# A two-layer graph attention kernel: its setup in another order, query and key weights first

## The reference

```python
q, k, v = (proj(Wq, bq), proj(Wk, bk), proj(Wv, bv))        # x @ W.T + b, in heads
scores = jnp.einsum('bhqd,bhkd->bhqk', q, k) / np.sqrt(D_HEAD)
mask = adj + jnp.eye(n, dtype=adj.dtype)[None] > 0
attn = jax.nn.softmax(jnp.where(mask[:, None], scores, -jnp.inf), axis=-1)
out = jnp.einsum('bhqk,bhkd->bhqd', attn, v)                 # then heads joined
h = x + out @ Wo.T + bo
x1 = (h - mu) * jax.lax.rsqrt(var + EPS) * gamma + beta
feat_proj = x1 @ fc_w.T + fc_b
logits = (feat_proj @ q_w.T + q_b) + (feat_proj @ k_w.T + k_b).swapaxes(2, 1)
masked = logits + (1.0 - adj) * NEG_INF
masked = jnp.where(masked >= 0, masked, LEAKY_SLOPE * masked)
y = jax.nn.softmax(masked, axis=-1) @ feat_proj + x1
```

## Time and profile before

| | |
|---|---|
| median of 3 runs | 985.23 us (985.12 to 985.61) |
| the profiled execution: its time / its span | 985.61 us / 983.4 us |
| PE / PEld busy | 932.2 us (95%) / 777.8 us (79%) |
| DVE / ACT / POOL busy | 768.7 (78%) / 796.1 (81%) / 300.5 us (31%) |
| HBM read, written | 52.44 MB, 8.39 MB |

### The profile page before, as it was taken

The page is one execution under the profiler, slowest core; times in us unless marked ns, Lnnn a source line. Parts: engine busy times, 40 slices in busy tenths (PEclk is TensorE's granted clock), DMA queues, the critical chain, the costliest instruction groups (busy, mean ns, idle before and its releaser), DMA issues. The chain is left out here.

```text
span 983.4 us, 22056 instructions
## 1 busy us (share of the span) xinstructions
PE 932.2 (95%) x7432; PEld 777.8 (79%) x7432; DVE 768.7 (78%) x2012; ACT 796.1 (81%) x1900; POOL 300.5 (31%) x408
## 2 busy tenths in 40 slices
PE   4498999999999999999999999999999999999966
PEld 3276888888888888888788888878887888888755
DVE  3287987979788797978878797888879797887832
ACT  2187988989888897988889798988989898897923
POOL 0002332334333233433214243432323343232441
PEclk8699999999999999999999999999999999999988
DMA  5576856666575666657476665737666564756100
GB/s 150 85 110 149 118 141 108 130 119 99 136 116 133 108 130 129 109 126 117 123 119 133 123 129 109 118 124 116 150 111 129 108 108 130 118 120 108 44 22 22
DMA packets 74430, 112.59 MB, mean 114 GB/s; under 512 B 6736, under 2 KB 33360, under 8 KB 74320
## 3 DMA queue, kind: packets, MB, share of 16 engines
q1 hardware_dynamic: 74320, 111.18, 58.8%
HBM read 52.44 MB, written 8.39 MB: 62 GB/s over the span
## 5 line engine op out<-in xcount | busy, mean ns | idle before, releaser
L912 DVE CUSTOM_DVE_ANT_0 sm_bank<-sm_bank,masks 128x512 f32<-128x512 f32 x512 | 352.3, 698 | 124.1 <-PE sm_bank L494 121.2
L679 ACT ACTIVATE e<-sm_bank,row_min 128x512 f32<-128x512 f32 x512 | 355.3, 696 | 41.9 <-DVE row_min L912 41.9
L504 PE MATMUL et_bank<-ident,e 128*128 128x128 f32 x2048 | 307.9, 272 | 3.2 <-DVE e_t L920 1.9
L504 PEld LDWEIGHTS et_bank<-ident,e 128*128 128x128 f32 x2048 | 251.6, 140 | 42.5 <-issue 7.3
L494 PE MATMUL sm_bank<-k_stack,q_stack 96*128 96x512 f32 x512 | 248.0, 485 | 13.5 <-DMA k_stack<-kt_lo 12.7
L671 ACT COPY e_t<-et_bank 128x512 f32<-128x512 f32 x272 | 161.0, 592 | 16.1 <-PE et_bank L504 14.2
L920 DVE COPY e_t<-et_bank 128x512 f32<-128x512 f32 x240 | 164.4, 685 | 11.8 <-PE et_bank L504 10.2
L494 PEld LDWEIGHTS sm_bank<-k_stack,q_stack 96*128 96x128 f32 x512 | 97.2, 190 | 43.5 <-issue 25.5
L443 PE MATMUL o_bank<-e_t,v 128*32 128x256 f32 x2048 | 123.8, 382 | 0.0
L476 PE MATMUL shared<-feat,z 128*128 128x256 f32 x512 | 121.6, 381 | 0.8 <-ACT z L621 0.8
L679 ACT ACTIVATION_READ_ACCUMULATOR e<-sm_bank,row_min 128x1 f32 x512 | 106.9, 209 | 0.0
(11 more groups left out here) (110 smaller groups left out, 1578.9 us busy)
## 6 DMA issues: line engine op xcount, KB each, us to landing
adj_in<-in_adj SPq DMA_DIRECT2D x32, 1024.0 KB, 5.3
q_stack<-qt_hi SPq DMA_DIRECT2D x64, 256.0 KB, 7.1
k_stack<-kt_hi SPq DMA_DIRECT2D x64, 256.0 KB, 7.2
x_in<-in_x SPq DMA_DIRECT2D x16, 512.0 KB, 6.4
q_stack<-qt_lo SPq DMA_DIRECT2D x32, 256.0 KB, 7.1
k_stack<-kt_lo SPq DMA_DIRECT2D x32, 256.0 KB, 11.1
h<-in_x SPq DMA_DIRECT2D x16, 512.0 KB, 3.9
out_y<-h SPq DMA_DIRECT2D x32, 256.0 KB, 6.8
```

What stands on the lines that cost most here:

```text
L504: last = nc.tensor.transpose(et_bank[n % TURNED][:, c * P:(c + 1) * P], e[:, n % ROOM, c * P:(c + 1) * P], ident[:, :])
L679: nc.scalar.activation(e[:, k, :], sm_bank[n % SCORED][:, :], ACT.Exp, scale=-1.0, bias=row_min[:, k:k + 1], accum_out=row_sum[:, g, qt, i ...
L912: nc.vector.tensor_tensor_reduce(bank[:, :], bank[:, :], mask[b % 2][:, qt * N:(qt + 1) * N], 1.0, -LOWEST, ALU.add, ALU.min, row_min[:, k ...
```

## The change

SP issues Wq and Wk first (counted in a semaphore of their own, qk_loaded), then x, then the four columns of bq and bk (bias_loaded), then adj; Wv, Wo, fc_w, kw_col, the other columns and the rows follow. PE, ACT and DVE make the parts of Wq and Wk and go straight on to the turns of x and the projections k0 and q0. All the rest of the setup becomes a function other_weights on each of the three engines, called in iteration -1 at step 17, behind q0. The setup now uses the banks of the scores, of the output and of the turned tiles in place of the two shared ones, since the projections need those. The wait of SP for PE's seventh setup signal moves behind the first stack transfers, and PE waits for the whole of the setup at the first scores.

```diff
 FIRST, LAST = -1, NB + 1
+FIRST_QK, AFTER_QK = 15, 17
...
         weights_loaded, cols_loaded, const_loaded = sem("weights_loaded"), sem("cols_loaded"), sem("const_loaded")
-        N_WEIGHTS, N_COLS, N_CONST = 6, 3, 12
+        qk_loaded, bias_loaded = sem("qk_loaded"), sem("bias_loaded")
+        N_QK, N_BIAS, N_WEIGHTS, N_COLS, N_CONST = 2, 4, 4, 3, 8
         ident_made = sem("ident_made")
+        setup_banks = [*sm_bank, o_bank, et_bank[1]]
         setup_pe, setup_act, setup_dve = sem("setup_pe"), sem("setup_act"), sem("setup_dve")
...
-            for k, w in enumerate((wq, wk, wv, wo)):
+            def load_weight(k, w, signal):
                 sp.dma_start(z[:, k, 0:N].rearrange("p (o i) -> p o i", o=DT),
-                             w.rearrange("(o p) i -> p o i", p=P)).then_inc(weights_loaded, 16)
+                             w.rearrange("(o p) i -> p o i", p=P)).then_inc(signal, 16)
+
+            load_weight(WQ, wq, qk_loaded)
+            load_weight(WK, wk, qk_loaded)
+            sp.dma_start(x_in[:, :, :], rows(x, 0)).then_inc(x_loaded.sem, 16)
+            for k, b in enumerate((bq, bk)):
+                for g in range(NG):
+                    sp.dma_start(bias_col[:, k, g:g + 1], b[g * P:(g + 1) * P].rearrange("(i d) -> d i", i=GH),
+                                 allow_slow_non_contiguous=True).then_inc(bias_loaded, 16)
+            sp.dma_start(adj_in[:, :, :], rows(adj, 0)).then_inc(adj_loaded.sem, 16)
+            load_weight(WV, wv, weights_loaded)
+            load_weight(WO, wo, weights_loaded)
             sp.dma_start(h[0][:, 0:DT, :], fc_w.rearrange("(o p) i -> p o i", p=P)).then_inc(weights_loaded, 16)
             sp.dma_start(kw_col[:, :], k_w.rearrange("a (g p) -> p (a g)", p=P),
                          allow_slow_non_contiguous=True).then_inc(weights_loaded, 16)
-            sp.dma_start(x_in[:, :, :], rows(x, 0)).then_inc(x_loaded.sem, 16)
 
             for col, b in ((bias_col[:, 2, :], bv), (gamma_col[:, :], gamma), (beta_col[:, :], beta)):
                 sp.dma_start(col, b.rearrange("(g p) -> p g", p=P),
                              allow_slow_non_contiguous=True).then_inc(cols_loaded, 16)
-            for k, b in enumerate((bq, bk)):
-                for g in range(NG):
-                    sp.dma_start(bias_col[:, k, g:g + 1], b[g * P:(g + 1) * P].rearrange("(i d) -> d i", i=GH),
-                                 allow_slow_non_contiguous=True).then_inc(const_loaded, 16)
-            sp.dma_start(adj_in[:, :, :], rows(adj, 0)).then_inc(adj_loaded.sem, 16)
             for row, b in ((gamma_row, gamma), (rest_row, beta), (bo_row, bo), (fcb_row, fc_b)):
...
             def iteration(t):
                 for s in range(TILES):
+                    if t == 0 and s == 0:
+                        sp.wait_ge(setup_pe, 7)
                     if (b := due(SP_AT, "adj", s, t)) is not None and b > 0:
                         sp.wait_ge(dve_done.sem, max(dve_done.all("mask", b - 1), dve_done.all("l_max", b - 2)))
...
 
-            sp.wait_ge(setup_pe, 7)
             program(iteration)
...
             pe.wait_ge(ident_made, 2)
-            pe.wait_ge(weights_loaded, 16 * N_WEIGHTS)
-            setup_banks = [*shared, *sm_bank][:5] + [o_bank]
-            for k in range(5):
+
+            def turn_weight(k):
                 for i in range(DT):
...
                         last = nc.tensor.transpose(setup_banks[k][:, (i * DT + o) * P:(i * DT + o + 1) * P],
                                                    src, ident[:, :])
                 last.then_inc(setup_pe, 1)
-            pe.wait_ge(setup_dve, 1)
...
-            pe.wait_ge(setup_dve, 9)
+
+            pe.wait_ge(qk_loaded, 16 * N_QK)
+            turn_weight(WQ)
+            turn_weight(WK)
+
+            def other_weights():
+                pe.wait_ge(weights_loaded, 16 * N_WEIGHTS)
+                pe.wait_ge(ident_made, 4)
+                for k in (WV, WO, FC):
+                    turn_weight(k)
+                pe.wait_ge(setup_dve, 4)
+                for i in range(DT):
...
+                last.then_inc(setup_pe, 1)
+                pe.wait_ge(setup_act, 5)
+                pe.wait_ge(setup_dve, 7)
+                for kt in range(DT):
+                    for n, part in enumerate((weight_hi, weight_lo)):
...
+                last.then_inc(setup_pe, 1)
 
...
@@ -506,6 +523,13 @@
 
             def iteration(t):
                 for s in range(TILES):
+                    if t == FIRST and s == FIRST_QK:
+                        pe.wait_ge(setup_dve, 3)
+                    if t == FIRST and s == AFTER_QK:
+                        other_weights()
+                    if t == 0 and s == 0:
+                        pe.wait_ge(setup_act, 7)
+                        pe.wait_ge(setup_dve, 10)
                     if (b := due(PE_AT, "at3", s, t)) is not None:
                         attend(3, b)
...
 
         @block.scalar
         def _(act):
-            banks = [*shared, *sm_bank]
-            for k in range(4):
+
+            def high_parts(k):
                 act.wait_ge(setup_pe, k + 1)
...
+                    last = nc.scalar.copy(weight_hi[:, k, :, :], setup_banks[k][:, :].rearrange("p (i o) -> p i o", i=DT))
                 last.then_inc(setup_act, 1)
-            act.wait_ge(setup_pe, 5)
-            nc.scalar.copy(scratch[:, 6, :], banks[4][:, :]).then_inc(setup_act, 1)
...
-            act.wait_ge(const_loaded, 16 * N_CONST)
-            act.wait_ge(setup_dve, 9)
+
+            high_parts(WQ)
+            high_parts(WK)
+            act.wait_ge(setup_dve, 3)
+
+            def other_weights():
+                high_parts(WV)
+                high_parts(WO)
+                act.wait_ge(setup_pe, 5)
+                nc.scalar.copy(scratch[:, 6, :], setup_banks[FC][:, :]).then_inc(setup_act, 1)
...
+                                                scale=gamma_col[:, i:i + 1])
+                last.then_inc(setup_act, 1)
 
...
             def iteration(t):
                 for s in range(TILES):
+                    if t == FIRST and s == AFTER_QK:
+                        other_weights()
                     if (b := due(ACT_AT, "v0", s, t)) is not None:
...
-            last.then_inc(setup_dve, 1)
-            banks = [*shared, *sm_bank]
-            for k in range(4):
+
+            def low_parts(k):
                 dve.wait_ge(setup_act, k + 1)
                 if k == WQ:
...
-
-            dve.wait_ge(const_loaded, 16 * N_CONST)
-            nc.vector.tensor_scalar(bias_col[:, 0, :], bias_col[:, 0, :], -SCALE, None, ALU.mult)
-            dve.wait_ge(setup_pe, 7)
-            nc.vector.tensor_tensor(bo_row[:, :], et_bank[0][:, 0:D], bo_row[:, :], ALU.add)
...
-            nc.vector.tensor_tensor(logit_bias[:, 3:4], logit_bias[:, 0:1], logit_bias[:, 1:2], ALU.add).then_inc(setup_dve, 1)
-            dve.wait_ge(setup_dve, 13)
+
+            low_parts(WQ)
+            low_parts(WK)
+            dve.wait_ge(bias_loaded, 16 * N_BIAS)
+            nc.vector.tensor_scalar(bias_col[:, 0, :], bias_col[:, 0, :], -SCALE, None, ALU.mult)\
+                .then_inc(setup_dve, 1)
+
+            def other_weights():
+                dve.wait_ge(weights_loaded, 16 * N_WEIGHTS)
+                dve.wait_ge(ident_made, 4)
+                for o in range(DT):
+                    last = nc.vector.tensor_scalar(scratch[:, 0, o * P:(o + 1) * P], scratch[:, 1, 0:P], kw_col[:, o:o + 1], None, ALU.add)
+                last.then_inc(setup_dve, 1)
...
+                last.then_inc(setup_dve, 1)
+                low_parts(WV)
+                low_parts(WO)
+                dve.wait_ge(setup_act, 6)
+                for i in range(DT):
...
+                last.then_inc(setup_dve, 1)
+
+                dve.wait_ge(const_loaded, 16 * N_CONST)
+                dve.wait_ge(setup_pe, 7)
+                nc.vector.tensor_tensor(bo_row[:, :], et_bank[0][:, 0:D], bo_row[:, :], ALU.add)
+                nc.vector.tensor_tensor(fcb_row[:, :], et_bank[0][:, D:2 * D], fcb_row[:, :], ALU.add).then_inc(setup_dve, 1)
+                dve.wait_ge(setup_dve, 10)
...
+                nc.vector.tensor_tensor(logit_bias[:, 0:2], logit_bias[:, 0:2], qkb[:, :], ALU.add).then_inc(setup_dve, 1)
+                dve.wait_ge(setup_dve, 13)
+                nc.vector.tensor_tensor(logit_bias[:, 3:4], logit_bias[:, 0:1], logit_bias[:, 1:2], ALU.add).then_inc(setup_dve, 1)
+                dve.wait_ge(setup_dve, 14)
 
...
@@ -922,6 +963,8 @@
 
             def iteration(t):
                 for s in range(TILES):
+                    if t == FIRST and s == AFTER_QK:
+                        other_weights()
                     if (b := due(DVE_AT, "fin1", s, t)) is not None:
...
             nc.gpsimd.memset(scratch[:, 1, 0:P], 0.0).then_inc(ident_made, 1)
-            pool.wait_ge(setup_dve, 10)
+            pool.wait_ge(setup_dve, 11)
```

(20 more changed lines are left out.)

81 lines of the change are left out of this document (38 added, 43 removed).

## The result

| | before | after |
|---|---|---|
| median of the runs, us | 985.42 (985.12 to 986.05, 4 runs) | 972.78 (971.64 to 973.66, 4 runs) |
| after over before | | 0.9872, 95% interval 0.9856 to 0.9887 |
| profiled execution, us (its span) | 985.61 (983.4) | 973.40 (971.2) |
| granted clock of TensorE, mean of the profiled execution | 0.981 | 0.989 |

The kernel is 1.3% faster: 12.6 us by the medians, 12.2 by the two profiled executions (985.61 - 973.40). The forecast was 971.8, and 972.1 for the profiled execution, which came out 1.3 above it.

What follows compares the result with a forecast made beforehand. TensorE is full in the steady part, so the start adds to the whole. Taking 13.5 us off the profiled 985.61 gives 972.1, 971.7 with the 0.38 lower median; stated 971.8, range 969.3 to 975.6 us.

Steps and rivals of the forecast that it cites:

- Direction and mechanism: Start of the kernel: K and Q ahead of other setup work, first stack issue 13.5 us earlier, carried to the end.
- Weights: PE waits for Wq and Wk alone: first transpose at 4.4 us, DVE's low parts done by 7.9, bias scaled by 8.1.
- x: x issued at 1.79 us, landing at 6.5 by Wo's row; 7.6 by its own time would make K 0.7 later.
- Biases: bq and bk columns ahead of adj land at 6.7 us, no delay taken; late bound 9.3, K 1.3 us later.
- K to stack: From K's start at 10.4 us to first stack issue at 17.5: 7.1 us as before, TensorE at 0.50, SP free.
- rival B: Warm TensorE: K and Q matmuls at 0.27 us at most, not 0.42, some 2 us more off, 969.6; chance 0.10.
- Stack: From first stack issue to first scores: 14.4 us kept as before, first scores at 31.9 us.
- Block: Deferred setup behind Q: DVE done by 26.4 us, POOL by 30.0, covered by the stack transfer with 1.9 us to spare.
- After the first scores: Order unchanged and steady PE full, so the shift is carried whole; TensorE's clock may vary it 2 us either way.
- C: Rival: cover too short, or biases and x late; 976.2 us by the block, 973.1 by late bias and x; chance 0.16.
- D: Rival: slower than before, last constant landing late ahead of q1's low part and masks; 988.5 us if landed at 43; chance 0.02.
- E: Rival: nothing gained, something unseen holds the first scores at 45 us; 985.2 us, chance 0.02.

Runs made afterwards that it cites:

- experiment 1: Kernel before with only SP's setup transfers in the new order, PE, ACT and DVE in the old order; 987.06 us median, ratio 1.0026.
- experiment 2: Changed kernel with SP's setup transfers in the order of before, the engines' new order kept; 973.9 us, ratio 0.9893.
- experiment 3: Changed kernel with old transfer order and other weights' work ahead of x's turns again; only DVE's constants wait and sums behind Q; 979.1 us, ratio 0.9934.
- experiment 8: Changed kernel once more, nothing altered; 971.65 us (970.01 to 974.36, 5 runs), ratio 0.9869.
- experiment 7: Changed kernel with query bias scaling moved behind DVE's xt_lo, ACT waiting for biases only ahead of K's high part, PE not; 971.69 us, ratio 0.9865.
- experiment 5: Changed kernel with 24 chained 128x512 copies on DVE in the deferred block, ahead of its wait for the constants; 976.22 us, one run.
- 4: Changed kernel with six chained 128x512 copies on DVE in the deferred block, ahead of its wait for the constants; 972.08 us, one run.
- 6: Changed kernel with SP waiting for the four bias transfers before issuing adj and everything behind it; 974.05 us, ratio 0.9884.
- experiment 10: Changed kernel with bias off the path, first stack's query columns split, and unread transposes and matmuls filling PE's waits before K and first scores; 964.41 us, ratio 0.9791.

## Why the prediction was right, and where it was off

**Direction and mechanism** held: K ahead of the rest, the constant's wait and the block taken from the path. Experiments 1 to 3 show it part by part.

**Weights**: first transpose at 4.4, measured 4.62; DVE's low parts were done by 8.04 (7.9).

**x**: 6.5 us, chosen from Wo's place in the stream over 7.6 from x's own time; the turns began at 7.08, 6.70 (experiment 8) and 6.38 (experiment 7). The profiled execution lies halfway between the two rows, the others nearer to Wo's.

**Biases**: "I take no delay" failed in the profiled execution, and by more than its bound: scaling ended at 10.65 for 8.1, where I had allowed 1.3 us. The step at fault is the choice of bounds: 2.4 and 5.0 us were single landings, taken as if they were the ends. In experiment 5 they were late by 0.9 us, in 4, 6, 7 and 8 in time within 0.2. The Trainium skill, "DMA: Bandwidth & Descriptors", section Specifications, speaks against small pieces; of when they are late its rule tells nothing, and no run here does.

**K to stack**: 7.1 us forecast, 6.7 measured (19.40 - 12.74), since the last of Q quickened. SP was free for it, though its setup issues ended at 16.2 and not at 14.0. In experiment 8 it was 4.6, which is rival B's case: warm matmuls, and 970.01 where B had said 969.6. Whether B comes depends on the execution, not on the kernel alone; 0.10 was too low for it, as it came up in the profiles of experiments 1, 3, 6 and 8. The Trainium skill, "TensorE: Matmul & The Clock Gate", section What's actually happening, has activity release the clock; experiment 10 agrees for K, without proof that the filling did it, and only in part for the scores.

**Stack**: 14.4 forecast, 14.1 measured, 14.0 and 14.4 in experiments 7 and 8, 13.4 in 4 and 15.4 in 6. The last constants landed 2.3 us behind the first stack issue, and no delay is seen from it.

**Block**: last DVE instruction by 26.4, POOL by 30.0, with a stack issue at 17.5; measured 27.12 and 29.87 with the issue at 19.40. Against the issue the block was 1.2 us (DVE) and 2.0 us (POOL) shorter than I had it, since I had put PE's bias products wholly behind DVE, which they overlapped (they began at 21.89, DVE's parts ended at 23.04), and q1 at the low level, where its matmuls came mostly 0.23 to 0.24 us apart. The cover has 3.6 us to spare, not 1.9.

**After the first scores**: ten matmuls at 0.50, as before; the shift was carried whole (11.9 us at the scores, 12.3 in the steady part). The sum: 2.3 us late at K by the bias, 0.4 back at Q, 0.3 back at the stack are the 1.6 by which the scores missed 31.9; 0.3 more comes back behind them, and 1.3 is what the profiled execution missed 972.1 by. C's mechanism was there (the bias), its price was in part taken back. That the total came so near is in part luck: the bias cost 2.3 us more than forecast, and 1.0 came back at Q, in the stack and behind the first scores, where I had forecast no gain. D and E fell: the last constant landed by 21.7 us. In experiment 8 DVE did wait 2.3 us for it, until 20.90, with 3.3 us of cover still left.

## What to carry to other kernels

Where the steady part is full, read the start backwards from the first instruction of the bound engine, and sort the setup work by what that chain needs: the rest belongs on the engines' queues behind it, under whatever transfer is waited for anyway. Reordering transfers without the engines' queues gained nothing here. Count the cover in dates, not in sums: idle time inside the moved block is cover too. After such a move the next term is on the same rows: here the stack's bytes, then the clock.

## What the runs showed of the hardware

- Small transfers have no one price: the two halves of bk landed 2.4 us after their issue before, 3.4 and 4.6 (medians) in two executions of the same kernel after, and the latest of them took 6.2.
- An execution of one unchanged kernel can start its K at 10.37 or 12.74 us and run K's matmuls at either level; its nine times lie between 970.01 and 974.36 us. An edit worth under 2 us, as experiment 7, can't be judged from one profile's time; dates on the chain can.
- The granted clock falls outside the setup too: 0.66 at 75 to 80 us in experiment 7, 1.00 there in the kernel after. Of the 3.4 us gained at the scores 1.8 were left at the first store in experiment 7, and 3.9 of 4.2 in experiment 8, with 1.00 in that stretch. Why the level fell in one and not in the other is not shown.
- The clock column may say 1.00 over a stretch in which the matmuls keep the low level's pace (13 to 17.1 us of the kernel after, 0.43 us a matmul): compare it with the distance of their starts.
